# Expert rows made in place, four buffers deep, with down products four units behind their gate products

## What is computed

```python
tidx, tw = _gate(x, gate_w, gate_bias)        # 8 of 64 experts per token, and their weights
w_dense = jnp.zeros((T, E), tw.dtype).at[jnp.arange(T)[:, None], tidx].add(tw)
def body(acc, ws):
    wg, wu, wdn, cw = ws
    hmid = jax.nn.silu(x @ wg) * (x @ wu)
    return (acc + cw[:, None] * (hmid @ wdn), None)
y, _ = jax.lax.scan(body, jnp.zeros_like(x), (We_gate, We_up, We_down, w_dense.T))
shared = jax.nn.silu(hidden_states @ Ws_gate) * (hidden_states @ Ws_up) @ Ws_down
return y + shared
```

## Time and profile before

| | us |
|---|---|
| median of 3 runs | 736.21 |
| lowest run | 736.17 |
| the profiled execution | 734.65 |
| its span, first to last instruction | 732.8 |

### The profile page before, as it was taken

One profiled execution on the slowest core, in us unless ns is written; L12 is line 12 of the kernel. 1 busy time (PEld: TensorE's weight loads), 2 busy tenths in 40 slices (PEclk: granted clock), 3 DMA queues, 4 the chain that ended last, 5 costly groups with the idle time before them and its releaser, 6 DMA issues.

```text
span 732.8 us, 15746 instructions
## 1 busy us (share of the span) xinstructions
PE 706.5 (96%) x5616; PEld 544.9 (74%) x5616; DVE 543.8 (74%) x1146; ACT 445.1 (61%) x857; POOL 424.5 (58%) x351
## 2 busy tenths in 40 slices
PE   7889899999999999999999999999999999999997
PEld 6666687677877778777787777777787777887885
DVE  4777769777697777886688866976778876876664
ACT  2877765576546855567455675557654675555553
POOL 2537686864465645565456644556455664566665
PEclk9999999999999999999999999999999999999999
DMA  7335774344543454445434353444344344444441
GB/s 267 89 118 153 220 135 125 103 125 133 116 134 103 132 117 117 132 108 151 108 111 120 121 152 105 129 106 139 103 129 138 91 151 111 109 129 141 127 133 44
DMA packets 66845, 92.93 MB, mean 127 GB/s; under 512 B 7888, under 2 KB 26768, under 8 KB 66768
## 3 DMA queue, kind: packets, MB, share of 16 engines
q1 hardware_dynamic: 61728, 85.90, 42.9%
q10 hardware_dynamic: 5040, 6.03, 2.5%
HBM read 88.37 MB, written 3.15 MB: 125 GB/s over the span
## 4 chain that ended last, share of the span: by engine, by line
PE 71%; DVE 12%; ACT 9%; issue 3%; POOL 3%; DMA 2%; SPq 0%; POOLq 0%; ACTq 0%; DVEq 0%
PE banks L992 68%; DVE act_w L959 4%; POOL hid_lo L637 2%; DVE hid L971 2%; ACT s_t L402 2%; ACT hid_hi L540 2%; ACT banks L528 1%; ACT L528 1%; PE banks L1072 1%; ACT L402 1%; DMA x_early<-in_x_feat 1%; DVE head_max L712 1%; DVE s_t L711 1%; ACT v_blk L389 1%; DMA cwb<-cw_scratch 1%
## 5 line engine op out<-in xcount | busy, mean ns | idle before, releaser
L637 POOL TENSOR_TENSOR hid_lo<-hid,hid_hi 128x512 fp32r<-128x512 f32 (+1 forms) x264 | 342.1, 1296 | 267.2 <-ACT hid_hi L540 265.4
L959 DVE TENSOR_TENSOR act_w<-banks,cwb 128x512 f32<-128x512 f32 x254 | 174.6, 687 | 127.5 <-ACT banks L528 121.5
L528 ACT ACTIVATE banks<-banks 128x512 f32<-128x512 f32 x254 | 147.3, 582 | 139.4 <-PE banks L992 136.8
L540 ACT CAST hid_hi<-hid 128x512 fp32r<-128x512 f32 (+1 forms) x264 | 162.6, 616 | 73.4 <-DVE hid L971 71.7
L971 DVE TENSOR_TENSOR hid<-act_w,banks 128x512 f32<-128x512 f32 (+1 forms) x264 | 181.3, 687 | 24.0 <-PE banks L992 1.4
L992 PE MATMUL banks<-c_hi,wg_hi 128*128 128x512 f32 x264 | 118.1, 447 | 2.9 <-DVE act_w L959 2.1
L992 PE MATMUL banks<-hid_hi,wd_hi 128*128 128x512 f32 (+1 forms) x264 | 107.0, 405 | 4.3 <-POOL hid_lo L637 4.0
L992 PE MATMUL banks<-hid_hi,wd_lo 128*128 128x512 f32 (+1 forms) x264 | 103.9, 393 | 0.0
L992 PE MATMUL banks<-c_lo,wg_hi 128*128 128x512 f32 x264 | 103.8, 393 | 0.0
L992 PE MATMUL banks<-hid_lo,wd_hi 128*128 128x512 f32 (+1 forms) x264 | 103.8, 393 | 0.0
L992 PE MATMUL banks<-c_hi,wg_lo 128*128 128x512 f32 x264 | 103.7, 393 | 0.0
(11 more groups left out here) (159 smaller groups left out, 798.4 us busy)
## 6 DMA issues: line engine op xcount, KB each, us to landing
cwb<-cw_scratch SPq DMA_DIRECT2D x254, 256.0 KB, 3.8
k_blk<-in_cond_w SPq DMA_DIRECT2D x112, 64.0 KB, 2.5
xf<-in_x_feat SPq DMA_DIRECT2D x8, 256.0 KB, 3.8
out_feat<-y ACTq DMA_DIRECT2D x8, 256.0 KB, 3.4
wg_raw<-in_we_gate SPq DMA_DIRECT2D x7, 256.0 KB, 4.6
wu_raw<-in_we_up SPq DMA_DIRECT2D x7, 256.0 KB, 4.7
wd_raw<-in_we_down SPq DMA_DIRECT2D x7, 256.0 KB, 4.9
xf<-in_x_tok SPq DMA_DIRECT2D x6, 256.0 KB, 2.7
```

The lines of the kernel that those rows point to most:

```text
L528: nc.scalar.activation(dst, gate_bank(p)[:, :], ACT.Silu).then_inc(S["silu_done"], 1)
L540: nc.scalar.copy(hid_hi[0:n, p % NH, :], hid[0:n, p % NH, :]).then_inc(S["hi_ready"], 1)
L637: nc.gpsimd.tensor_sub(hid_lo[0:n, p % NH, :], hid[0:n, p % NH, :], hid_hi[0:n, p % NH, :].bitcast(F32)).then_inc(S["lo_ready"], 1)
L959: nc.vector.tensor_mul(act_w[:, p % NH, :], gate, weight)\
```

## The change

act_w is gone. The weighted row is written into hid, and the second product of DVE reads and writes hid. hid, hid_hi and hid_lo have NH = 4 buffers, numbered by `slot(b, p)` = (b * 33 + p) % 4, which runs on from block to block. With NH = 4 the down product of unit p-4 stands in unit p, total at the head of unit 3, the store of y at unit 4. Before the weighted row of p DVE waits for lo_ready of unit p-4, since POOL reads that buffer; the silu of the 64-row unit waits for lo_ready too. stats, pick, c_hi1 and c_lo1 change their places in SBUF. The selection of the pooling borrows hid in place of act_w. Cut to its core:

```diff
-        hid_hi, hid_lo = sb("hid_hi", [P, 3, TOK], F32R), sb("hid_lo", [P, 3, TOK], F32R)
+        NH = 4
         c_hi1, c_lo1 = sb("c_hi1", [P, TOK], F32R), sb("c_lo1", [P, TOK], F32R)
+        hid_hi, hid_lo = sb("hid_hi", [P, NH, TOK], F32R), sb("hid_lo", [P, NH, TOK], F32R)
...
-        NH = 3
         cwb = sb("cwb", [P, NCW, TOK])
-        act_w = sb("act_w", [P, NH, TOK])
         hid = sb("hid", [P, NH, TOK])
...
-        Y_STORED = 3
+        Y_STORED = 4
...
+        def slot(b, p):
+
+            return (b * UNITS + p) % NH
...
-                    act.wait_ge(S["hid_ready"], b * UNITS + p - NH + 1)
-                    nc.scalar.activation(act_w[0:F, p % NH, :], gate_bank(p)[0:F, :], ACT.Silu)\
+                    act.wait_ge(S["lo_ready"], b * UNITS + p - NH + 1)
+                    nc.scalar.activation(hid[0:F, slot(b, p), :], gate_bank(p)[0:F, :], ACT.Silu)\
                         .then_inc(S["silu_done"], 1)
...
-                    nc.vector.tensor_mul(act_w[:, p % NH, :], gate, weight)\
+                    if b * UNITS + p >= NH:
+                        dve.wait_ge(S["lo_ready"], b * UNITS + p - NH + 1)
+                    nc.vector.tensor_mul(hid[:, slot(b, p), :], gate, weight)\
                         .then_inc(S["weighted"], 1)
...
-                nc.vector.tensor_mul(hid[0:n, p % NH, :], act_w[0:n, p % NH, :], up).then_inc(S["hid_ready"], 1)
+                nc.vector.tensor_mul(hid[0:n, slot(b, p), :], hid[0:n, slot(b, p), :], up).then_inc(S["hid_ready"], 1)
```

More of the change, by code:

```diff
@@ L100, in adaln_attention_moe @@
             wd_raw = sb_early("wd_raw", [P, UNITS, D])
+            stats = sb_early("stats", [P, 8, NSEQ // SPT])
+            pick = sb_early("pick", [P, 2, 2, P])
             x_early = sb_early("x_early", [P, 6, TOK])
-            pick = sb_early("pick", [P, 2, 2, P])
-            stats = sb_early("stats", [P, 8, NSEQ // SPT])
         wg_lo, wu_lo = sb("wg_lo", [P, UNITS, P], F32R), sb("wu_lo", [P, NPAIR, P], F32R)
         wd_lo = sb("wd_lo", [P, UNITS, D], F32R)
-        hid_hi, hid_lo = sb("hid_hi", [P, 3, TOK], F32R), sb("hid_lo", [P, 3, TOK], F32R)
+        NH = 4
         c_hi1, c_lo1 = sb("c_hi1", [P, TOK], F32R), sb("c_lo1", [P, TOK], F32R)
+        hid_hi, hid_lo = sb("hid_hi", [P, NH, TOK], F32R), sb("hid_lo", [P, NH, TOK], F32R)
         wg_hi, wu_hi = sb("wg_hi", [P, UNITS, P], F32R), sb("wu_hi", [P, NPAIR, P], F32R)
@@ L163, in adaln_attention_moe @@
         tiles32 = "p a (n l) -> p (a n) l"
-        sel = act_w[:, 0:2, :].rearrange(tiles32, l=SEQ)
+        sel = hid[:, 0:2, :].rearrange(tiles32, l=SEQ)
         pool_act = [s_t[:, 0, :], s_t[:, 1, :], rt[:, :, :].rearrange("p a n -> p (a n)")]
@@ L526, in silu @@
                 if p < NPAIR:
-                    dst = act_w[:, p, :] if b == 0 and p < 2 else gate_bank(p)[:, :]
+                    dst = hid[:, p, :] if b == 0 and p < 2 else gate_bank(p)[:, :]
                     nc.scalar.activation(dst, gate_bank(p)[:, :], ACT.Silu).then_inc(S["silu_done"], 1)
                 else:
-                    act.wait_ge(S["hid_ready"], b * UNITS + p - NH + 1)
-                    nc.scalar.activation(act_w[0:F, p % NH, :], gate_bank(p)[0:F, :], ACT.Silu)\
+                    act.wait_ge(S["lo_ready"], b * UNITS + p - NH + 1)
+                    nc.scalar.activation(hid[0:F, slot(b, p), :], gate_bank(p)[0:F, :], ACT.Silu)\
                         .then_inc(S["silu_done"], 1)
@@ L539, in rounded @@
                 n = P if p < NPAIR else F
-                nc.scalar.copy(hid_hi[0:n, p % NH, :], hid[0:n, p % NH, :]).then_inc(S["hi_ready"], 1)
+                nc.scalar.copy(hid_hi[0:n, slot(b, p), :], hid[0:n, slot(b, p), :]).then_inc(S["hi_ready"], 1)
             def unit(b, p, par, following, last, prev):
@@ L636, in unit @@
                 n = P if p < NPAIR else F
-                nc.gpsimd.tensor_sub(hid_lo[0:n, p % NH, :], hid[0:n, p % NH, :],
-                                     hid_hi[0:n, p % NH, :].bitcast(F32)).then_inc(S["lo_ready"], 1)
+                nc.gpsimd.tensor_sub(hid_lo[0:n, slot(b, p), :], hid[0:n, slot(b, p), :],
+                                     hid_hi[0:n, slot(b, p), :].bitcast(F32)).then_inc(S["lo_ready"], 1)
                 if not prev and p in SPLITS:
@@ L953, in unit @@
                         dve.wait_ge(S["cwb_ps"], p + 1)
-                        gate, weight = act_w[:, p, :], G[p]
+                        gate, weight = hid[:, p, :], G[p]
                     else:
@@ L1243, in down @@
                     pe.wait_ge(S["y_ready"], b + 1)
-                three(Y[:, :], wd_hi[0:n, p, :], wd_lo[0:n, p, :], hid_hi[0:n, p % NH, :], hid_lo[0:n, p % NH, :],
+                three(Y[:, :], wd_hi[0:n, p, :], wd_lo[0:n, p, :], hid_hi[0:n, slot(b, p), :], hid_lo[0:n, slot(b, p), :],
                       p == 0, p == UNITS - 1).then_inc(S["down_done"], 1)
```

## The result

The changed kernel takes 728.07 us in the median of four runs (727.32 to 730.47), the kernel before 736.19 beside it; ratio 0.9899, 95% interval 0.9879 to 0.9919. (One of the four runs of the kernel before took 2394 us; the other three took 735.98 to 736.21.) Run again in more rounds (e1) it takes 727.6 against 736.45, ratio 0.989 (0.9868 to 0.9913). That is 8 to 9 us, against 9.3 forecast. Both intervals lie clear of 1, so a gain of about 1% is shown, though the prediction held 2% to be the least that a measurement of this kernel can tell.

A forecast was written before the change was run, and what follows sets the result against it. PE's start-to-start spacing was taken as the bound, with DVE close behind in routing; 4.2 + 3.6 + 1.5 = 9.3 us off the profiled 734.65 gives 725.4, plus 1.56 for the median, 727.0 us. Range 724.0 to 731.5.

The forecast's parts named there:

- 1.56 us added for the median: Whole run: the median of the kernel before, 736.21, lies 1.56 us above its profiled execution; added to 725.4, giving 727.0.
- (c): Unit 9, exponential stage: PE's wait for hid_lo of unit 6 goes; 0.7 us in each of six blocks, 4.2 us.
- (b): Unit 3, score wait: with total behind the second head_max, PE's idle goes; 0.6 us in six blocks, 3.6 us.
- score wait not relieved: Rival, unit 3: (b) brings 0 and the median becomes 730.5 us; chance 0.15.
- (d): Routing, units 17 to 27: PE's hid_lo stalls shrink; 0.3 us in blocks 1, 3, 5, 0.2 in others; 1.5 us.
- up(0) waits for hid(32) as before: Start of the next block: the chain from gate(28) to hid(32) moves as a whole; the wait stays, worth nothing.
- PE waits for hid instead: Sign of being wrong: PE's removed waits are replaced by waits for hid; no size given.
- Buffers and rows in place at nothing: All units: hid replaces act_w with the same shapes, 0.69 us each, cost 0; act_w's three rows pay for the added ones.
- The new wait on DVE at nothing: Before each weighted row: the lo_ready wait lies under DVE's preceding operation; taken as 0, from above 5 us.
- The rival of 2 to 3 us: Rival: the new wait on DVE shows, 2 to 3 us lost, 729.5 us; chance 0.06.
- Slower by routing retimed against POOL: Rival: routing operations on DVE meet POOL's hid_lo more often; 1.0 us lost per block, 742.2 us; chance 0.04.
- Block 0 at nothing: Block 0: gate(28) waits for POOL's split of the up weights; no PE time saved before it comes through; gain nothing.

The follow-up runs named there:

- e11: Changed kernel with down products three units behind in units 5 to 11, four elsewhere; 727.4 us, ratio 0.9871.
- e12: e10 with unit 5 taking two down products, units 6 to 11 three behind, down(6) behind up(9), unit 12 none; 721.67 us, ratio 0.9817.
- e3: Changed kernel with total back in unit 2, which gets two down products, unit 3 none; 738.15 us, ratio 1.0027.
- e2: Changed kernel with down products three units behind, total and store back; rows in place, four buffers and new wait stay; 737.32 us, ratio 1.0013.
- e8: Changed kernel with three more satisfied waits on DVE before each weighted row; 729.39 us, ratio 0.9908.
- e10: Changed kernel with nine small products in block 0's unit 3 and block 1's category values read before the units; 724.56 us, ratio 0.9829.
- e7: Changed kernel with only block 1's category values read before the units; 727.03 us, ratio 0.9875.
- e9: Changed kernel with nine small products in unit 3 of block 0; 726.77 us, ratio 0.9864.
- e5: The kernel before, unchanged, run again for a second profile of its opening; one run, 736.46 us.
- e6: Changed kernel with 28 small products in unit 3 of block 0; 728.61 us, ratio 0.9894.

## Why the prediction was right

The time, 727 to 728, and the sum, 9.3 us, came out; from gate(28) of block 0 on the traces give 9.3, so the sum came out by its terms and not by luck; less sure was the 1.56 us added for the median, which rests on one profile. Step by step, with the table above:

- **(c), unit 9: 0.7 a block; measured 0.73 and 0.71** (9 to 10). Right, and up(9) and the transpose behind it are not late, as the slack worked out said. What the prediction didn't see is that a second idle time, 0.25 us with its restart 0.41, lies one unit earlier. It costs the forecast nothing, but e11 shows that (c) was one of two ways to the same gain, and e12 that both can be had.
- **(b), the scores: 0.6 a block; measured 0.42 + 0.22 = 0.64 and 0.39 + 0.19 = 0.58.** Right in size and cause: total follows the second head_max, and e3 puts it back and brings the wait back. The rival *score wait not relieved* is out; up(2) doesn't hold row 2. The working holds in its parts too: from the first head_max to the second takes 2.81 us, 0.88 less (0.9 forecast), and the scores start 0.31 after head_max ends (327.92 - 327.53 = 0.39 forecast), where they start 0.05 after it when they wait.
- **(d), the routing: 0.3 in odd blocks, 0.2 in even ones; measured 0.44 - 0.14 = 0.30 and 0.17.** The cap of 0.34 that the prediction took from weighted row 25 is to be seen: 0.44 is gained up to unit 25 and 0.14 given back before gate(27). The even blocks, guessed, came close.
- **up(0) waits for hid(32) as before, worth nothing:** right. *PE waits for hid instead* was one of the signs of being wrong, and the profile after has three such waits (0.23 us, at 234.51, 404.28 and 574.04), all at up(0). They are the wait that the prediction left as it is. Before, down(30) of the old block started 0.37 us after the gate product ahead of it (402.62 to 402.99) instead of 0.23, and hid(32) was late behind it all the same; now down(29) isn't late, and the whole wait is seen as idle time of up(0). From gate(0) to up(0) of block 4 takes 1.79 us before (402.15 to 403.94) and 1.78 after (402.50 to 404.28). What the later down product wins there is given back at once.
- **Sum:** 3 x (0.64 + 0.73 + 0.30) + 3 x (0.58 + 0.71 + 0.17) = 9.4 us, taking block 6 as an even one.
- **Buffers and rows in place at nothing:** right by e2, whose interval reaches from a gain of 0.4 to a loss of 2.2 us (and whose loss holds the new wait too).
- **The new wait on DVE at nothing:** about 0.3 us by e8, so not quite nothing. DVE's waiting for lo_ready was a sign of being wrong too; there is one such wait of 0.61 us in the whole run, at 650.07 us, and none in e1. The rival of 2 to 3 us is out.
- **Slower by routing retimed against POOL:** out. The first 128x64 comparison takes 1082 ns in the mean, as 1081 before, so no meeting was added:

```profile
L763 DVE TENSOR_TENSOR rt<-rt 128x64 f32<-128x64 f32 x8 | 8.7, 1082 | 0.0
```

  The trace of the kernel before speaks for that row being a wait for POOL. The comparison takes 0.23 us in the opening, where POOL is idle (45.79), 0.71 at 111.22, where hid_lo has run for 0.7 us already, and 1.27 to 1.31 in the six places where hid_lo starts just ahead of it; those seven times it ends 0.07 to 0.09 us after hid_lo does. One of the six, in the timelines of POOL and DVE:

```profile
370.83 1.29 POOL L637 TENSOR_TENSOR hid_lo<-hid,hid_hi 128x512 fp32r<-128x512 f32 x1 [0.76 <-ACT hid_hi L540]
370.94 1.27 DVE L760 TENSOR_TENSOR rt<-rt 128x64 f32<-128x64 f32 x1
```

  No run here moved one against the other, so it is not shown by an experiment.
- **Block 0 at nothing: open.** Of the 9.3 us the medians show 8.1 and 8.85, so 0.5 to 1.2 us may have gone there. The opening took 92.4 and 91.9 us after, 89.1 and 90.9 before, but e2, with the old order, 91.7. It differs between executions of one kernel by as much as between the two, and the sum holds without it. The reason given is too strong, though, that no PE time saved before the split comes through: e10 shortens exactly this stretch to 87.3 us (e12 to 88.2), and as much arrives at the end. PE still waits 1.1 us for the split in e10, as in e1, so the split moved with the rest. e10 keeps PE's clock whole and relieves SP's queue; which of the two reaches the split is not shown, and e7 and e9, with one each, gained less than half as much.
- **The tail:** the idle time before the down product of unit 31 falls from 1.02 to 0.51 us, and gate(32) to the end is as long as before, as the prediction said. The timeline of PE after:

```profile
723.26 0.50 PE L997 MATMUL banks<-hid_hi,wd_hi 128*128 128x512 f32 x1 [0.51 <-POOL hid_lo L640]
```

The marks that the prediction named (8 waits to 2, the block to 84.9) came out: 84.43 and 85.33 have the mean 84.88. One didn't: the one wait for head_max left is 0.56 us long in the profile of after and 2.45 in e1, not 1.4. In before and e5 it is 1.42 and 2.81, so it varies between executions in both kernels.

## What to carry over

Look up each wait in the timeline of the engine that bounds the kernel, and ask where its instructions could stand instead: a product moved by one unit was worth 0.7 us a block, extra buffers alone nothing. When one wait is gone, look one unit to each side for the next: it may be as large, and may be filled by the same product moved the other way, or by another. A run that undoes one part has to be read in the timeline before its time is believed: e11 put the wait back and lost nothing, and only its neighbour told why.

## What the runs showed of the hardware

PE's clock fell inside a busy kernel after short idle times, and not after each. Behind the twelve waits of 0.43 to 0.56 us in blocks 1 to 6 of the kernel before, the granted clock is 1.00 in every window. In e3 the same 1.2 us idle stands before the scores of six blocks; in two of them (at 330.59 and 590.48 us) the 512-column products of the next units are 0.43 us apart for some 3 us, at a granted clock of 0.50, in the other four they aren't. In block 0 it fell after 2.45 us idle (e1, at 62.93), 2.81 (e5) and 1.50 (e2), and not after 1.42 (before, at 63.50). In all it fell behind that wait in eight of the ten profiles without small products in it, and in none of the four with them (e6, e9, e10, e12), though in e9 1.92 us of idle time were left behind the nine. Behind the 2.15 us wait of gate(9) in block 0 it fell in twelve of the fourteen profiles (in that of before it is 0.50 from 82 to 84 us), and not in those of after and e10. So waits like these may be paid twice in this kernel, and single executions differ by it. The Trainium skill, "TensorE: Matmul & The Clock Gate" (Part 1: The HAM clock gate), gives 426.7 ns from start to start of 512 columns at 1.2 GHz and 215.7 at 2.4; the rows agree with the first (0.43) and lie a little above the second (0.23).

SP issues the loads of `k_blk` (64 KB each) in fours; four took 1.90 us at 83.70 and 2.93 at 87.08 in one execution, and the load of cwb behind them went out a microsecond later. SP's queue in the profile of after:

```profile
83.70 1.90 SPq L302 DMA_DIRECT2D k_blk<-in_cond_w  x4
...
87.08 2.93 SPq L302 DMA_DIRECT2D k_blk<-in_cond_w  x4
90.13 0.52 SPq L333 DMA_DIRECT2D cwb<-cw_scratch  x1
```

PE waits 2.00 us for att at 96.38 in that execution; in e1 the fours take 1.90 to 1.93 there and PE has no such wait. But e9's fours take 1.90 to 1.95, and PE waits 1.45 us for att all the same. So the slow four is not shown to be the cause.
